# Attention over four images: the search for maxima follows a concave line beside the scores, the next batch's projections are asked for later

## The chip, the cores and the metric

One core of a Trainium2 chip runs the whole program. The metric is the time of the device in microseconds for one execution of the kernel. Five engines work side by side: PE (matrix products), DVE (vector), ACT (scalar functions), POOL and SP, each with its own queue of instructions that it takes in order; semaphores order them among each other.

## What is computed

The program is a network of four layers over four images of 128 channels and 48 x 48 places. The change is in the last attention, which the reference computes so, for B = 4, T = 2304 tokens, 4 heads of 32 channels, all in float32:

```python
qkv = jnp.einsum('btc,oc->bto', x, qkv_w) + qkv_b
q, k, v = jnp.split(qkv, 3, axis=-1)
q, k, v = (heads(q), heads(k), heads(v))
att = jnp.einsum('bhqd,bhkd->bhqk', q, k) * scale
att = jnp.where(causal, att, -jnp.inf)
att = jax.nn.softmax(att, axis=-1)
out = jnp.einsum('bhqk,bhkd->bhqd', att, v)
out = out.transpose(0, 2, 1, 3).reshape(B, T, C)
return jnp.einsum('btc,oc->bto', out, out_w) + out_b
```

x is the layer-normalised stream, and the result is added to it.

## The kernel before, in words

`program` runs six phases one after the other: a selective scan (a), a deformable convolution (b), a linear-attention stack (c), two mixtures of experts (d, f), and between them `attention` (e), which alone is touched. Phases share nothing but X, the stream, which stays on chip.

**Tiling of the attention.** Queries go in blocks n = 0 to 19, five to a batch b (j = 0 to 4, 512 queries wide, the last 256). Keys go in tiles t of 128. A block j has 4(j+1) key tiles (18 for j = 4), of which the last four (two) lie on the diagonal and are narrower. Everything is in the channel layout: a score tile holds 128 keys by up to 512 queries, for four heads in two pairs `hp`, each pair a `slot` of PSUM. There are three slots (two banks each), besides `pO` (outputs) and `pZ` (row sums).

**Kinds of steps.**
- `ln`, `var`, `qk`, `v`: layer norm and projections of group g (512 tokens) of batch b, with `square`, `rstd`, `xn`, `q_out`, `k_out`, `v_out` that take them out of PSUM.
- `most`: the search. For 128 queries i and 512 keys kc, PE forms the scores of two heads the other way round (queries in partitions), and DVE takes their maximum over the keys (`most_out`, L3277; on the diagonal first a mask, L3272). `peak` (L3285) joins the parts, `neg` (L3183) transposes them, and `neg_out` gives minus the maximum of each query, the *level* of block n.
- `score`: four matmuls of K times Q and four that add the level (`e_neg`, `e_ones`); it needs two free slots, and for t = 0 the level of its block (`neg_out`). `masked` on the diagonal (L3291), then `exp` on ACT (L3374) writes P.
- `av` adds into `pO`, `sum` into `pZ`; of four tiles ahead of the diagonal, the first two are added by POOL (`fold`, L3398) so that one `sum` serves both. `rec`, `on`, `proj`, `residual` end the block.

So the level of a block has to be there before its first score tile; the search of a block may run any time after its projections, at most NR = 4 blocks ahead.

**What sets the order.** The order of all steps is worked out when the program is built, by `Line`: jobs (`main` for scores, `outputs`, `others` for projections and search, `projections` for the ends of blocks) are generators on a model clock with a cost for each kind (COST), and each step that a job puts is appended to `ph.order`. Every engine then issues its part of that order, with waits on semaphores. What PE finds first in its queue it must do first.

`others` goes through `plan`: for each block n from 1 the pieces of its search (`max_units`), with projections of the next batch spread among them, and then `neg` n. `done` counts the items gone through. `scores` holds a tile back until `done` has come to `due(n, t)`, which before is the share of the score columns so far, times the weights of the whole plan, less SLACK = 2 items. That binds the scores to the search, but not the search to the scores: `others` runs on as slots permit. Projections of batch b+1 stand in `plan` among the search of blocks j = 1 to 3 (two groups each).

```python
while done[0] < due(n, t) and not stuck[0]:
    yield
```

All matmuls of the phase are issued in the helper `mm`, so that they share line 3129 and are told apart by their tiles: `e_slot<-e_K,e_Q` is the search, `e_slot<-e_Q,e_K` and `e_slot<-e_neg,e_ones` the scores, `e_pO<-e_P,e_V` the outputs, `e_pZ<-e_P,e_ones` the sums, `e_slot<-X,cst` and `e_slot<-e_sqr,cst` the norm, `e_slot<-e_xn,e_w` Q and K, `e_slot<-e_w,e_xn` V, `e_slot<-e_On,e_w` the output projection. Each float32 matmul stands as two instructions in the trace.

Of the kernel before, what the change touches and what calls it, by code (L numbers as in the profile page):

```python
# [14 lines left out]
B, C, HH, WW = 4, 128, 48, 48  # L15
L = HH * WW
# [4 lines left out]
class Phase:  # L21
# [17 lines left out]
    def put(self, kind, *key):  # L39
        self.total[kind] = self.total.get(kind, 0) + 1  # L40
        self.rank[kind, key] = self.total[kind]
        self.order.append((kind, key))
# [11 lines left out]
class Line:  # L54
# [22 lines left out]
    def spawn(self, work):  # L77
        self.jobs.append([self.now[0], work, -1, self.rank[0]])
# [24 lines left out]
    def until(self, kind, *key):  # L103

        while not self.emitted(kind, *key):
            yield
        if self.ready[kind, key] > self.now[0]:
            self.now[0] = self.ready[kind, key]
            yield
# [2717 lines left out]
def attention(nc, A, X, K):  # L2827
    ph = Phase(nc, "e")
    S, upto = ph.sem, ph.upto
    SCALE = float(1.0 / np.sqrt(32))  # L2830
    NT, QB, NP, NR, SLACK = L // 128, 512, 12, 4, 2
    w = ph.sb("w", [128, 384 + 128 + 4])
    cm = ph.sb("cm", [128, 2, 128])
    ones = ph.sb("ones", [128, 128])
# [10 lines left out]
    neg = ph.sb("neg", [128, NR, QB])  # L2845
# [7 lines left out]
    blocks = [(b, j) for b in range(B) for j in range(5)]  # L2853

    def width(j):
        return min(QB, L - j * QB)

    def tiles(j):
        return range(4 * j, 4 * j + width(j) // 128)

    def first(j, t):

        return max(t - 4 * j, 0) * 128

    def key_chunk(i, kc):
        return kc * QB, min((i + 1) * 128, kc * QB + QB)
# [12 lines left out]
    def take(kind, *key, us=None):  # L2879
        while True:  # L2880
            first = min(pairs, default=None, key=lambda x: x[0])
            if len(pairs) <= wanted[0]:
                yield
            elif first[0] > now[0]:
                now[0] = first[0]
                yield
            else:
                break
        pairs.remove(first)
        _, place[kind, key], freed[kind, key] = first  # L2890
        put(kind, *key, us=us)
# [5 lines left out]
    def spread(us, z):  # L2897
        return us * z / QB + .1

    def scores(n, t):  # L2900

        j = blocks[n][1]
        z = width(j) - first(j, t)
        if t == 0:
            yield from until("neg_out", n)
        if tile_no[n, t] >= NP // 2:
            n0, t0 = tile_at[tile_no[n, t] - NP // 2]
            yield from until("av", n0, t0)
            if paired(blocks[n0][1], t0):
                yield from until("fold", n0, t0 // 4 * 4 + 1)  # L2910
            else:
                yield from until("sum", n0, t0)
        while done[0] < due(n, t) and not stuck[0]:
            yield
        wanted[0] = 2
        while len(pairs) < 2 or max(x[0] for x in pairs[:2]) > now[0]:
            if len(pairs) >= 2:
                pairs.sort()
                now[0] = max(now[0], pairs[1][0])
            yield  # L2920
        wanted[0] = 0
        pairs.sort()
        for hp in range(2):
            _, place["score", (n, t, hp)], freed["score", (n, t, hp)] = pairs.pop(0)
        put("score", n, t, us=spread(1.7, z))
        for hp in range(2):
            spawn(weights(n, t, hp, z))
        yield

    def weights(n, t, hp, z):  # L2930
        j = blocks[n][1]
        if t >= 4 * j:
            put("masked", n, t, hp)
            yield
        put("exp", n, t, hp, us=spread(.9, z))
        give(("score", (n, t, hp)), ("exp", (n, t, hp)))
# [44 lines left out]
    def normed(b, g):  # L2981
        put("square", b, g)
        yield
        put("var", b, g)
        yield
        put("rstd", b, g)
        yield
        put("xn", b, g)
        give(("ln", (b, g)), ("xn", (b, g)))

    def query_key(b, g):
        aside("q_out", b, g)
        put("k_out", b, g)
        give(("qk", (b, g)), ("q_out", (b, g)), ("k_out", (b, g)))
        yield

    def out(taker, kind, *key, us=None):
        put(kind, *key, us=us)
        give(taker, (kind, key))
        yield  # L3000

    def extra(kind, *key):
        if kind == "ln":
            b, g = key
            if gno(b, g) >= 2:
                yield from until("v", *divmod(gno(b, g) - 2, 5))
            yield from take("ln", *key)
            spawn(normed(*key))
        elif kind == "qk":
            yield from until("xn", *key)  # L3010
            if key[0] >= 2:
                stuck[0] = True
                yield from until("score", 5 * (key[0] - 1) - 1, NT - 1)
                yield from until("av", 5 * (key[0] - 1) - 1, NT - 1)
                stuck[0] = False
            yield from take("qk", *key)
            spawn(query_key(*key))
        elif kind == "v":
            yield from take("v", *key)
            spawn(out(("v", key), "v_out", *key))  # L3020
        elif kind == "most":
            n, i, kc = key
            b, j = blocks[n]
            a0, a1 = key_chunk(i, kc)
            if kc == 0:
                yield from until("q_out", b, j)
                yield from until("k_out", b, j)
            for hp in range(2):
                yield from take("most", n, i, kc, hp, us=spread(.4, a1 - a0))
                spawn(out(("most", (n, i, kc, hp)), "most_out", n, i, kc, hp,  # L3030
                          us=spread(1.0, a1 - a0) + .43 * (kc == i // 4)))
            if kc == i // 4:
                spawn(top(n, i))
        elif kind == "neg":
            n = key[0]
            j = blocks[n][1]
            for i in tiles(j):
                yield from until("peak", n, i)
            if n >= NR:
                stuck[0] = True  # L3040
                yield from until("score", n - NR, tiles(blocks[n - NR][1])[-1])
                stuck[0] = False
            yield from take("neg", n)
            spawn(out(("neg", key), "neg_out", n))
        yield
# [8 lines left out]
    def top(n, i):  # L3054
        for kc in range(i // 4 + 1):
            for hp in range(2):
                yield from until("most_out", n, i, kc, hp)
        put("peak", n, i)

    def max_units(n):  # L3060
        b, j = blocks[n]
        return [("most", n, i, kc) for i in tiles(j) for kc in range(i // 4 + 1)]

    def others():
        for g in range(5):
            yield from extra("ln", 0, g)
            if g:
                yield from extra("qk", 0, g - 1)
                yield from extra("v", 0, g - 1)
        yield from extra("qk", 0, 4)  # L3070
        yield from extra("v", 0, 4)
        for m in max_units(0):
            yield from extra(*m)
        yield from extra("neg", 0)
        for e in plan:
            yield from extra(*e)
            done[0] += 1

    def gno(b, g):
        return 5 * b + g  # L3080


    plan = []
    for n, (b, j) in enumerate(blocks[1:], 1):
        ahead = []
        if b + 1 < B and 1 <= j < 4:
            ahead += [(kind, b + 1, g) for g in range(2 * j - 2, min(2 * j, 5)) for kind in ("ln", "qk", "v")]
        todo = max_units(n)
        for k, piece in enumerate(ahead):
            todo.insert((k + 1) * (len(todo) + k) // (len(ahead) + 1), piece)  # L3090
        plan += todo + [("neg", n)]
    done, stuck = [0], [False]
    tile_at = [(n, t) for n, (b, j) in enumerate(blocks) for t in range(tiles(j)[-1] + 1)]
    tile_no = {key: k for k, key in enumerate(tile_at)}

    def paired(j, t):
        return t < 4 * j and t % 4 < 2

    WEIGHT = {"ln": 3.0, "qk": 2.0, "v": 1.0, "neg": 1.0}
    work = [sum(width(blocks[m][1]) - first(blocks[m][1], u) for m, u in tile_at[:k]) for k in range(len(tile_at) + 1)]  # L3100
    rest = [sum(WEIGHT.get(e[0], 2.2) for e in plan[:k]) for k in range(len(plan) + 1)]

    def due(n, t):
        share = work[tile_no[n, t]] / work[-1] * rest[-1]
        return max(sum(x <= share for x in rest) - 1 - SLACK, 0)

    line.run((0, main()), (0, outputs()), (0, others()), (0, projections()))

# [293 lines left out]


PHASES = (("a", layer0), ("b", layer1), ("c", layer2a), ("d", experts2), ("e", attention), ("f", experts3))


# [139 lines left out]
```

## Time and profile before

| | |
|---|---|
| time, median of 3 runs | 10961.17 us (10953.19 to 10961.48) |
| the profiled execution | 10953.31 us, its span 10951.5 us |
| instructions | 166018 |
| busy over the span | PE 84%, DVE 70%, ACT 55%, POOL 51% |
| the attention | 9415.3 to 10717.4 us of the span |

The times are those of whole executions. Busy shares are those of the span from the first to the last instruction. The profile also gives the clock that PE was granted, as a share of its full 2.4 GHz; the two levels are 0.5 (1.2 GHz) and 1.

### The profile page before, as it was taken

What the parts mean: (1) busy time and instruction counts of PE and PEld (TensorE: products, weight loads), DVE (VectorE), ACT (ScalarE), POOL (GpSimd) and SP (SyncE); (2) the same over time, 40 slices, a digit from 0 to 9 for tenths busy, and PEclk for the clock granted to TensorE, in tenths of its full rate; (3) what the DMA queues carried; (4) which work ended last, traced back from release to release, by engine and by line L of the source; (5) the groups of instructions that cost most, each with busy time, mean ns of one, the idle gap of its engine ahead of it and who ended that gap; (6) DMA issues with size and microseconds to landing.
All of it is one profiled execution on the core that took longest, in us unless ns stands there. A gap on an engine that the chain in (4) does not pass through costs nothing. (4 is left out here: it accounts for less than half of the span.)

```text
span 10951.5 us, 166018 instructions
## 1 busy us (share of the span) xinstructions
PE 9227.2 (84%) x59866; PEld 4819.9 (44%) x59866; DVE 7622.5 (70%) x8779; ACT 6061.1 (55%) x12476; POOL 5534.4 (51%) x3721
## 2 busy tenths in 40 slices
PE   7888888888888776677798998988989988799897
PEld 3333333333333333566555555555555554333334
DVE  5999999999999996566556665555665653444633
ACT  4666666767666664111356666666666665233233
POOL 5888889889888885666333323222323320011010
PEclk8999999999999998888889999999999999899898
DMA  2222222222222223666300000000000001200003
GB/s 72 76 77 78 80 78 79 79 78 80 78 80 78 79 77 97 193 195 196 102 2 2 4 5 1 4 1 5 4 1 5 1 10 42 94 1 1 1 1 142
DMA packets 259107, 623.72 MB, mean 57 GB/s; under 512 B 26279, under 2 KB 114447, under 8 KB 255992
## 3 DMA queue, kind: packets, MB, share of 16 engines
q1 hardware_dynamic: 203672, 438.27, 12.2%
q0 software_dynamic: 51840, 169.91, 5.2%
q8 instruction: 486, 7.96, 0.3%
q10 hardware_dynamic: 2784, 4.92, 0.1%
q14 instruction: 325, 2.66, 0.1%
HBM read 572.09 MB, written 40.90 MB: 56 GB/s over the span
## 5 line engine op out<-in xcount | busy, mean ns | idle before, releaser
L978 POOL TENSOR_TENSOR a_dBu<-a_du,a_Bs 128x960 f32<-128x960 f32 (+1 forms) x1280 | 2714.5, 2144 | 222.8 <-DVE a_H L750 202.5
L750 DVE TENSOR_TENSOR_SCAN a_H<-a_pA,a_dBu 128x962 f32<-128x962 f32 (+1 forms) x1280 | 2652.6, 2072 | 107.9 <-ACT a_pA L919 54.7
L919 ACT ACTIVATE a_pA<-a_delta,a_al 128x480 f32<-128x480 f32 (+1 forms) x2560 | 1624.8, 639 | 1148.8 <-DVE a_H L750 1143.9
L541 PE MATMUL a_pY<-a_H,cst 128*128 128x480 f32 (+1 forms) x5120 | 2213.5, 554 | 34.4 <-ACT a_Y L936 34.1
L758 DVE TENSOR_TENSOR a_H<-a_H,a_pC 128x960 f32<-128x960 f32 (+1 forms) x1280 | 1393.8, 1089 | 84.3 <-PE a_pC L541 83.0
L541 PEld LDWEIGHTS a_pY<-a_H,cst 128*128 128x128 f32 x5120 | 976.3, 193 | 707.0 <-issue 541.3
L541 PE MATMUL a_pC<-a_stk,a_sel 96*128 96x480 bf16 (+1 forms) x1280 | 471.6, 368 | 512.3 <-DVE a_H L758 504.1
L3398 POOL TENSOR_TENSOR e_P<-e_P 128x1024 f32<-128x1024 f32 (+1 forms) x80 | 151.8, 1918 | 1437.8 <-ACT e_P L3374 1437.8
L1089 POOL DMA_INDIRECT b_gath<-b_tab,b_idx x648 | 613.5, 947 | 392.1 <-issue 176.1
L2459 POOL TENSOR_TENSOR c_KF<-c_KF,c_dg 128x1056 f32<-128x1056 f32 x192 | 386.3, 2013 | 670.7 <-DVE c_MX L2219 670.3
L3374 ACT ACTIVATE e_P<-e_slot 128x1024 f32<-128x1024 f32 (+1 forms) x464 | 347.5, 796 | 657.0 <-PE e_slot L3129 588.5
L541 PEld LDWEIGHTS a_pC<-a_stk,a_sel 96*128 96x128 bf16 x1280 | 124.5, 97 | 1250.5 <-DVE a_H L758 1067.1
L1909 PE MATMUL c_P<-c_U,c_W 128*128 128x384 f32 x1536 | 582.5, 532 | 66.7 <-DVE c_mr L2264 38.5
L1141 PE MATMUL b_pS<-cst,b_gath 128*128 128x128 f32 x2592 | 374.4, 301 | 261.9 <-issue 198.0
L2411 ACT ACTIVATE c_G<-c_P,c_be 128x384 f32<-128x384 f32 x768 | 434.3, 581 | 177.9 <-PE c_P L1909 149.3
L3277 DVE TENSOR_REDUCE e_part<-e_slot 128x2 f32<-128x1024 f32 (+3 forms) x400 | 417.2, 1068 | 165.9 <-PE e_slot L3129 159.7
L1909 PE MATMUL c_P<-c_G,c_W 128*128 128x384 f32 x1536 | 520.9, 493 | 0.1
L2297 DVE SCALAR_TENSOR_TENSOR X<-c_P,c_be,X 128x384 f32<-128x384 f32 x192 | 118.2, 615 | 569.9 <-PE c_P L1909 569.7
L2448 POOL TENSOR_TENSOR c_t<-c_t 128x384 f32<-128x384 f32 x192 | 194.5, 1013 | 620.1 <-DVE c_t L2215 619.5
L2206 DVE SCALAR_TENSOR_TENSOR c_t<-c_P,c_be,c_sincos 128x384 f32<-128x384 f32 x576 | 335.5, 610 | 228.5 <-PE c_P L1909 226.3
L1141 PEld LDWEIGHTS b_pS<-cst,b_gath 128*128 128x128 f32 x2592 | 341.6, 211 | 296.6 <-issue 265.1
L2244 DVE TENSOR_REDUCE c_KS<-c_KF 128x264 f32<-128x1584 f32 x128 | 375.5, 2949 | 109.3 <-ACT c_KF L2370 109.2
(468 smaller groups left out, 18043.8 us busy)
## 6 DMA issues: line engine op xcount, KB each, us to landing
a_Bs<-a_brows SPq DMA_DIRECT2D x512, 480.0 KB
a_Bs<-a_brows SPq DMA_DIRECT2D x128, 384.0 KB
d_W<-in_d_w SPq DMA_DIRECT2D x32, 1024.0 KB, 7.5
f_W<-in_f_w SPq DMA_DIRECT2D x32, 1024.0 KB, 7.8
b_tab<-b_TT SPq DMA_DIRECT2D x32, 576.0 KB
b_gath<-b_tab,b_idx POOLq DMA_INDIRECT x648
a_zt<-a_sz SPq DMA_DIRECT2D x36, 256.0 KB
a_sz<-a_zt SPq DMA_DIRECT2D x16, 480.0 KB
```

The source lines that it names most:

```text
L541: return pe.matmul(out, lhsT, rhs, start=start, stop=stop, skip_group_check=True)
L750: v.tensor_tensor_scan(span(H[:, g % NH, :], g), factors(g), span(dBu[:, g % ND, :], g), 0.0, ALU.mult, ALU.add).then_inc(S(kind), 1)
L758: v.tensor_tensor(inner(H[:, g % NH, :], g), inner(H[:, g % NH, :], g), pC[:, 0:z].unsqueeze(1).broadcast_to([128, 2, z]), ALU.mult).then_ ...
L919: s.activation(pA[:, k, at:at + z], delta[:, u % 2, h, 0:z], ACT.Exp, scale=al[:, o + 2 * d, h, n:n + 1]).then_inc(S(kind), 1)
L978: g.tensor_tensor(inner(dBu[:, i % ND, :], i), du[:, u % 2, :, 0:z], Bs[:, p % NB, i % 2, 0:z].unsqueeze(1).broadcast_to([128, 2, z]), ALU ...
L1089: g.indirect_dma_start(out=gath[:, n % NG, t, :], out_offset=None, in_=tab[b], in_offset=bass.IndirectOffsetOnAxis(ap=idx[:, b % 2, j * 9 ...
L1141: m = pe.matmul(pS[:, place[kind, key], (t % 4) * 128:(t % 4 + 1) * 128], gath[:, n % NG, t, q * 128:(q + 1) * 128], ident, start=q == 0, ...
L1909: return pe.matmul(out, lhsT, rhs, start=start, stop=stop, skip_group_check=True)
L2244: v.tensor_reduce(KS[:, i, :], KF[:, :, i, :, :].rearrange("p c g m -> p (g m) c"), AX.X, ALU.add).then_inc(S(kind), 1)
L2411: s.activation(G[:, c % 2, j, :], half("up", n, c // 2 * 2, 0)[:, j, 0:CH], ACT.Gelu, bias=bias(n, 3 + j)).then_inc(S(kind), 1)
L2459: g.tensor_tensor(KF[:, c, :, :, :], KF[:, c, :, :, :], dg[:, c % 2, :].rearrange("p (i g) -> p i g", i=4).unsqueeze(3).broadcast_to([128, ...
L3277: v.tensor_reduce(part[:, n % NR, i - 4 * j, 2 * hp:2 * hp + 2, kc], sl[:, :, 0:z], AX.X, ALU.max).then_inc(S(kind), 1)
```

## The change

It is in the planner alone; what the steps do and the buffers are as before.

- Each level n has a latest point: EARLY = 1024 score columns before its block begins, by which the plan up to `neg` n has to be done (`corners`). `path` is the concave line from the origin over these points (from each point on to the next with the steepest rise). `due` reads it in place of the straight share.
- Scores wait until `done` is at least `due` less SLACK, as before, and now `others` waits while `done` is more than `due` plus SLACK (`reached` holds the `due` of the tile in hand).
- Projections of batch b+1 stand in the plan among the search of blocks j = 3 (groups 0 to 2) and j = 4 (groups 3 and 4).

```diff
-    NT, QB, NP, NR, SLACK = L // 128, 512, 12, 4, 2
+    NT, QB, NP, NR, SLACK, EARLY = L // 128, 512, 12, 4, 2, 1024
...
         z = width(j) - first(j, t)
+        reached[0] = due(n, t)
         if t == 0:
...
-        while done[0] < due(n, t) and not stuck[0]:
+        while done[0] < reached[0] - SLACK and not stuck[0]:
             yield
...
         for e in plan:
+            while done[0] > reached[0] + SLACK:
+                yield
             yield from extra(*e)
             done[0] += 1
...
-        if b + 1 < B and 1 <= j < 4:
-            ahead += [(kind, b + 1, g) for g in range(2 * j - 2, min(2 * j, 5)) for kind in ("ln", "qk", "v")]
+        if b + 1 < B and j >= 3:
+            ahead += [(kind, b + 1, g) for g in ((0, 1, 2), (3, 4))[j - 3] for kind in ("ln", "qk", "v")]
...
-    done, stuck = [0], [False]
+    done, reached, stuck = [0], [0], [False]
...
+    opened = [plan.index(("neg", n)) + 1 for n in range(1, len(blocks))]
+    corners = [(max(work[tile_no[n, 0]] - EARLY, 0), rest[k]) for n, k in enumerate(opened, 1)]
+    path, at = [(0, 0)], (0, 0)
+    while at[1] < rest[-1]:
+        at = max((p for p in corners if p[1] > at[1]), key=lambda p: ((p[1] - at[1]) / max(p[0] - at[0], 1), p[1]))
+        path.append(at)
+
     def due(n, t):
-        share = work[tile_no[n, t]] / work[-1] * rest[-1]
-        return max(sum(x <= share for x in rest) - 1 - SLACK, 0)
+        share = np.interp(work[tile_no[n, t]], [x for x, _ in path], [y for _, y in path])
+        return max(sum(x <= share for x in rest) - 1, 0)
```

How it moves the work on PE is seen in two places. A row is a run of equal matmuls; x2 of `e_slot<-e_K,e_Q` is one piece of search (two heads), x4 two pieces.

The first is block 14 (batch 2, j = 4), from its first score tile. Before:

```order
8292 L3129 MATMUL e_slot<-e_Q,e_K 128x256 x4
8293 L3129 MATMUL e_slot<-e_neg,e_ones 128x256 x4
8294 L3129 MATMUL e_pO<-e_P,e_V 32x128 x4
8295 L3129 MATMUL e_slot<-e_K,e_Q 128x512 x2
8296 L3129 MATMUL e_pZ<-e_P,e_ones 32x128 x4
8297 L3129 MATMUL e_slot<-e_K,e_Q 128x512 x10
8298 L3129 MATMUL e_pO<-e_P,e_V 32x256 x4
8299 L3129 MATMUL e_slot<-e_K,e_Q 128x128 x4
8300 L3129 MATMUL e_slot<-e_K,e_Q 128x512 x12
8301 L3129 MATMUL e_slot<-e_K,e_Q 128x256 x4
8302 L3129 MATMUL e_slot<-e_K,e_Q 128x512 x12
8303 L3129 MATMUL e_slot<-e_K,e_Q 128x384 x4
```

The same place after the change:

```order
8305 L3139 MATMUL e_slot<-e_Q,e_K 128x256 x4
8306 L3139 MATMUL e_slot<-e_neg,e_ones 128x256 x4
8307 L3139 MATMUL e_pO<-e_P,e_V 32x128 x4
8308 L3139 MATMUL e_slot<-e_K,e_Q 128x512 x2
8309 L3139 MATMUL e_pZ<-e_P,e_ones 32x128 x4
8310 L3139 MATMUL e_slot<-e_K,e_Q 128x512 x2
8311 L3139 MATMUL e_slot<-e_Q,e_K 128x256 x4
8312 L3139 MATMUL e_slot<-e_neg,e_ones 128x256 x4
8313 L3139 MATMUL e_slot<-e_K,e_Q 128x384 x2
8314 L3139 MATMUL e_pO<-e_P,e_V 32x256 x4
8315 L3139 MATMUL e_slot<-e_K,e_Q 128x384 x2
8316 L3139 MATMUL e_pO<-e_P,e_V 32x256 x4
```

The run of 32 pieces behind the first score tile is gone; two pieces stand there, and two behind the next.

The second is block 8 (batch 1, j = 3), which before holds no search at all:

```order
7902 L3129 MATMUL e_slot<-e_Q,e_K 128x512 x4
7903 L3129 MATMUL e_slot<-e_neg,e_ones 128x512 x4
7904 L3129 MATMUL e_pO<-e_P,e_V 32x128 x4
7905 L3129 MATMUL e_pZ<-e_P,e_ones 32x128 x4
7906 L3129 MATMUL e_slot<-e_Q,e_K 128x512 x4
7907 L3129 MATMUL e_slot<-e_neg,e_ones 128x512 x4
7908 L3129 MATMUL e_pO<-e_P,e_V 32x512 x4
7909 L3129 MATMUL e_slot<-e_On,e_w 128x512
7910 L3129 MATMUL e_slot<-e_Q,e_K 128x512 x4
```

After:

```order
7891 L3139 MATMUL e_slot<-e_Q,e_K 128x512 x4
7892 L3139 MATMUL e_slot<-e_neg,e_ones 128x512 x4
7893 L3139 MATMUL e_pZ<-e_P,e_ones 32x128 x4
7894 L3139 MATMUL e_slot<-e_K,e_Q 128x512 x2
7895 L3139 MATMUL e_slot<-e_xn,e_w 128x512 x2
7896 L3139 MATMUL e_slot<-e_Q,e_K 128x512 x4
7897 L3139 MATMUL e_slot<-e_neg,e_ones 128x512 x4
7898 L3139 MATMUL e_slot<-e_K,e_Q 128x512 x2
7899 L3139 MATMUL e_pO<-e_P,e_V 32x512 x4
7900 L3139 MATMUL e_slot<-e_K,e_Q 128x512 x2
7901 L3139 MATMUL e_slot<-e_On,e_w 128x512
7902 L3139 MATMUL e_pO<-e_P,e_V 32x512 x4
```

Search and the projections of batch 2 now stand between its score tiles. The search there is that of blocks 9 to 11.

## Rows read from the trace of the kernel before

**Rows 1.** The page: span, and busy time by engine.
```profile
span 10951.5 us, 166018 instructions
PE 9227.2 (84%) x59866; PEld 4819.9 (44%) x59866; DVE 7622.5 (70%) x8779; ACT 6061.1 (55%) x12476; POOL 5534.4 (51%) x3721
```

**Rows 2.** Windows (stretch, length, busy: PE, PEld, DVE, ACT, POOL; PEclk, DMA): attention.
```profile
9415.30:10717.40 1302.10, 1182.99 (x9122) 455.60 (x9122) 583.09 (x843) 436.74 (x625) 151.75 (x80) 0.92 0.01 1
```

**Rows 3.** Windows: blocks 0-3, 4, 5-7, 10-15, cut at first exponentials.
```profile
9464.10:9749.30 285.20, 256.60 (x1722) 91.67 (x1724) 142.57 (x202) 89.09 (x118) 27.96 (x12) 0.92 0.00 1
9749.30:9788.80 39.50, 37.68 (x563) 20.24 (x563) 3.51 (x8) 20.20 (x39) 9.96 (x8) 1.00 0.01 2
9788.80:10015.10 226.30, 201.45 (x1234) 74.23 (x1236) 137.46 (x193) 59.03 (x84) 13.95 (x6) 0.90 0.00 1
...
10110.70:10551.40 440.70, 402.10 (x2768) 152.19 (x2772) 252.82 (x350) 115.10 (x168) 37.92 (x20) 0.88 0.00 1
```

**Rows 4.** Windows: blocks 16 (j=1), 17 (j=2), 18 (j=3), without search.
```profile
10551.40:10578.70 27.30, 25.65 (x254) 9.24 (x257) 4.50 (x10) 14.19 (x19) 4.67 (x2) 1.00 0.01 2
10578.70:10620.80 42.10, 40.05 (x374) 13.70 (x374) 4.50 (x10) 21.88 (x27) 9.34 (x4) 1.00 0.00 1
10620.80:10676.80 56.00, 53.55 (x494) 18.07 (x494) 4.50 (x10) 29.59 (x34) 14.00 (x6) 1.00 0.01 1
```

**Rows 5.** Timeline of PE (start, length); and the tile e_slot: transposes.
```profile
9703.19 1.07 PE L3129 MATMUL e_pO<-e_P,e_V 128*32 128x512 f32 x8
9704.07 1.04 PE L3129 MATMUL e_pZ<-e_P,e_ones 128*32 128x512 f32 x8
9705.05 1.13 PE L3129 MATMUL e_slot<-e_sqr,cst 128*128 128x512 f32 x2
9706.10 1.07 PE L3129 MATMUL e_pZ<-e_P,e_ones 128*32 128x512 f32 x8
...
L3183 PE MATMUL e_slot<-cst,e_peak x72: 272/273/475, 9456.0 to 10549.1; 128*128 128x128 f32 x72
```

**Rows 6.** Groups of DVE in the attention (busy us, mean ns | idle before).
```profile
L3277 DVE TENSOR_REDUCE e_part<-e_slot 128x2 f32<-128x1024 f32 (+3 forms) x400 | 417.2, 1068 | 165.9 <-PE e_slot L3129 159.7
L3272 DVE TENSOR_TENSOR e_slot<-e_slot,e_cm 128x256 f32<-128x256 f32 x144 | 61.2, 425 | 44.9 <-PE e_slot L3129 44.3
```

**Rows 7.** Windows: the run of 17 in block 6, that of 32 in block 14.
```profile
9870.90:9899.00 28.10, 24.28 (x121) 9.62 (x118) 22.38 (x30) 4.20 (x8) 0.00 (x0) 0.88 0.00 1
10436.00:10478.50 42.50, 40.80 (x171) 16.66 (x170) 38.43 (x46) 2.31 (x4) 0.00 (x0) 0.60 0.00 1
```

**Rows 8.** Waits in 9418 to 10725 (us in total, times, longest).
```profile
PEld e_slot L3129 <- DVE e_part L3277: 206.0, 241, 2.5
PE e_slot L3129 <- DVE e_part L3277: 41.3, 83, 1.6
```

**Rows 9.** Windows: block 6 tiles 0-6, its twin; block 12 tiles 0-4, its twin.
```profile
9830.10:9870.90 40.80, 38.33 (x288) 14.70 (x290) 19.48 (x30) 16.68 (x21) 4.66 (x2) 1.00 0.01 1
10551.40:10576.20 24.80, 23.18 (x230) 8.30 (x233) 4.29 (x10) 13.43 (x17) 4.67 (x2) 1.00 0.01 1
10219.90:10250.50 30.60, 27.87 (x192) 9.41 (x194) 12.85 (x15) 10.81 (x13) 4.65 (x2) 1.00 0.00 1
10578.70:10598.30 19.60, 17.99 (x158) 5.84 (x158) 1.44 (x2) 10.78 (x12) 4.67 (x2) 1.00 0.00 1
```

**Rows 10.** Timeline of PE: one search piece between output and row sum.
```profile
9602.69 1.07 PE L3129 MATMUL e_pO<-e_P,e_V 128*32 128x512 f32 x8
9603.69 1.13 PE L3129 MATMUL e_slot<-e_K,e_Q 32*128 32x512 f32 x4
9604.75 1.06 PE L3129 MATMUL e_pZ<-e_P,e_ones 128*32 128x512 f32 x8
```

**Rows 11.** Windows: tile 3 of block 6 and of block 16.
```profile
9846.80:9853.70 6.90, 6.90 (x56) 2.65 (x52) 1.78 (x3) 2.58 (x4) 0.00 (x0) 1.00 0.01 2
10562.60:10566.90 4.30, 4.30 (x40) 1.35 (x44) 0.48 (x2) 1.94 (x2) 0.00 (x0) 1.00 0.00 0
```

## Prediction

> **What bounds the kernel now.** I read the page first: span and busy shares [rows 1]. The time of the profiled execution is 10953.3 us, its span 10951.5. The change touches only the attention, whose instructions run from 9415.3 to 10717.4, 1302.1 us, 12% of the span [rows 2]. There PE is busy 1183.0 us, DVE 583.1, ACT 436.7, POOL 151.8, and PE's granted clock is 0.92 on average. So PE sets the pace, but not at its full clock. Between the two levels of 1.2 and 2.4 GHz, a mean of 0.92 is 16% of the phase at 1.2 GHz, about 210 us.
>
> Then I cut the phase at the start of the first exponential of each query block [rows 3]. Three stretches hold all search for maxima after the lead-in; between and behind them stand blocks of scores alone. Without search PE has clock 1.00 and DVE nearly nothing to do. With search DVE works for half the time or more and the clock is 0.92, 0.90 and 0.88. The work is bunched: the search runs far ahead, then stops.
>
> **Price of the search now.** My unit is one search piece of 512 keys for two heads. The 400 reductions of the phase are 342 units (175104 columns over 512, counted over the PE's order), 3584 of those columns in the lead-in, so 335 units behind it. The three stretches last 285.2 + 226.3 + 440.7 = 952.2 us. The same blocks without search take 27.3 us (j=1), 42.1 (j=2), 56.0 (j=3) [rows 4], 39.5 (j=4) [rows 3]. A block j=0 nowhere stands alone; going by columns at the price of j=1, which is 8.2 ns, its 1280 would take 10.5 us, and smaller blocks pay more per column, so I take 12. Blocks 0 to 3: 137.4; 5 to 7: 81.4; 10 to 15: 188.9; sum 407.7. That leaves 544.5 us. In them lie the projections of batches 1 to 3. A group's matmul of 512 columns holds PE some 1.0 us (9705.05 to 9706.10; I take V's four small ones as one) [rows 5], five of them to a group, 4.5 groups to a batch: 13.5 x 5.0 = 68 us. The 19 groups of transposes of the levels (up to four of 0.27 us that overlap, [rows 5]) I put at 0.6 each, 11 us. The search then costs 544.5 - 68 - 11 = **466 us, 1.39 us a unit**.
>
> **Where that price comes from.** In a long run of search DVE is the pace: 417.2 us of reductions and 61.2 of masks [rows 6] over 342 units are 1.40 us a unit. Measured: the run of 17 pieces that ends block 6 takes 28.1 us [rows 7] against 2.5 in block 16 (27.3 of [rows 4] less 24.8 of [rows 9]); less 5.1 for the projections, transposes and output that lie in it, 20.5 us for 15 units, 1.37. That of 32 in block 14 takes 42.5; less 2.2 for its score tile (39.5 us for 18) and 1.0 for the output projection, 39.3 for 29 units, 1.36 [rows 7]. DVE is busy 22.4 and 38.4 us in them, and the clock is 0.88 and 0.60. PE waits for DVE's reductions 206.0 us before weight loads and 41.3 before matmuls [rows 8]. What stands behind a run pays too, since its score matmuls still run at the low clock.
>
> **Price of a spread piece.** Now stretches in which at most five pieces stand between two score tiles, against the same tiles of batch 3 [rows 9]. Block 6, tiles 0 to 6: 40.8 against 24.8, 16.0 more. In it are the matmuls of ln, of var twice, Q, K and V (6.0), and the output projection has moved out of it (1.0): 11.0 us for 10.5 units, 1.05. Block 12, tiles 0 to 4: 30.6 against 19.6, 11.0 more, with half-width var, Q and K for 1.5 and again 1.0 moved out: 10.5 for 9 units, 1.17. Together 21.5 / 19.5 = **1.10**. The clock is 1.00 in both although they hold 0.26 and 0.29 units per us. The single piece shows why: from 9603.69 to 9604.75 it holds PE 1.06 us between an output matmul and a row sum [rows 10], and its reduction on DVE (1.07 us on average, [rows 6]) lies beside other work.
>
> **The change, part by part.** No engine gets an instruction more or less. (1) `due` follows the concave line through the latest points at which each level must be ready, and `others` holds back beyond SLACK. By the PE's order, 41 of 68 gaps of the old program that hold search have at most four pieces, but runs of eight or more take 218.5 units. The new one has 151 gaps with search, none of seven to nine pieces, three of ten with 26.5 units, and 306 units in gaps of one to six. 81 score tiles have none, where 164 had. The lead-in takes 9.5 units instead of 7. (2) The projections of the next batch are asked for with the search of blocks j=3 and j=4, which comes well ahead of their scores. They keep their matmuls. I cost them at nothing more: by the order, the last V of a batch stands some 27 score tiles ahead of its first use, and ACT has room (busy 29.6 of 56.0 us in a pure block, [rows 4]). If that cover went, each group would hold the search for its chain of ln, square, var, rstd, xn, some 5 us, four times at worst. (3) The new wait of `others` is one of the planner, not of the chip; what stands behind it is the search of later blocks. Its risk is a level that is ready too late: the new order puts the transposes at least 1280 columns before their block (384 for block 1), over two tiles and 6 us, against a chain reduction - peak - transposes - copy of about 3 us. Before, six blocks had them directly ahead of their first scores. I take 0 for this, -10 to +10 as bounds.
>
> Sum after: 306 x 1.10 = 337, 26.5 x 1.40 = 37, together 374, against 466: -92. The lead-in, where nothing hides it, +3. **-89 us**, so 10864 for the profiled execution. The median of the runs shown is 10961.2, 8 above it: **10872**. Bounds of the price: 1.18, about that of the second stretch, gives -65; 0.95 gives -135: two pieces of different heads that run side by side would hold PE as long as one, 0.53 each, and 0.95 is what comes out if a fifth of them do.
>
> The order also costs something. PE changes between 32-row and 32-column tiles of the array more often: 806 changes of shape instead of 708. From an output matmul to a row sum of the same shape it is 0.88 us (9703.19 to 9704.07, [rows 5]), from an output matmul to a search piece 1.00 (9602.69 to 9603.69, [rows 10]). The Trainium skill, TensorEngine Tiling (Array Packing), Tiling Modes, says that changing the tiling mode drains the engine. The trace agrees with some 0.1 us; by that rule 98 more changes would be about 10 us, and the sum -79. I leave it out, since the stretches that give 1.10 have such changes themselves.
>
> **The clock.** From 10436.0 to 10478.5 PE is busy 40.8 of 42.5 us and has 0.60 [rows 7]; in 10551.4 to 10578.7 it is busy 25.7 of 27.3 and has 1.00 [rows 4]. So busy time alone does not keep the clock. The pure stretches of [rows 3] have 1.00 throughout, the falls lie where search is, and the runs have them most. I expect the 210 us at 1.2 GHz to shrink to about 70. The Trainium skill, TensorE: Matmul & The Clock Gate, Part 1, tells of a clock that is held down by default and that activity releases; taken as busy time, it would deny that this change helps the clock, which is the first rival.
>
> **Rivals.** (a) The clock stays low as long as now. What speaks for it: spread or bunched, a search piece fills half of the array. Against it: both stretches of [rows 9]. The 140 us that I let go would stay at half clock, and work bound by PE gives half of it back: -89 + 70 = -19, 10942, no change. Chance 0.07. (b) Slower: slots. A score tile needs two of three slots at once, and each piece put before it holds one until DVE has reduced it. A single piece can so cost more than one in a run: from 9846.8 to 9853.7 one piece and V take 6.9 us against 4.3 in block 16 [rows 11], less 1.0 for V, 1.6 us for the unit. If all 306 cost that the sum is 490 + 37 + 3 = 530, +64: 11025. The change stops paying at 1.39 and is slower by over 0.2% from 1.46. Against it: the stretches of [rows 9] have such pieces in them. Chance 0.05. (c) More gain: pieces side by side and the clock at 1.00 throughout, 0.95 a unit, -135: 10826. Chance 0.10. (d) That the planner's order hardly changes is excluded by the two orders.
>
> **How the numbers follow.** My forecast has 0.78, at 10872 with 10835 to 10925 as its own bounds. A measurement of this kernel tells about 0.2%, 22 us, from no change. Faster by more: 0.78 + 0.10 = 0.88; within 0.2%: 0.07; slower: 0.05. For 8 in 10 the range takes in half of (c) and ends below (a): 10828 to 10935.
>
> **What would show it.** The attention lasts 1195 to 1235 us; its clock is 0.96 or more; DVE is busy 583 us again; the last stretches without search, of batch 3, become longer (they get search), while blocks 14 and 15 shrink from 79.0 and 36.4 us; PE's waits for reductions fall from 247.3 us (206.0 and 41.3) to under 120. Wrong would be a mean clock of 0.92 again (rival a), or PE's waits for DVE as long as now at clock 1.00 (rival b).

## The result, and the profile after

Five runs each, on one chip: before 10961.48 us (10953.19 to 10972.68), after 10896.53 us (10882.21 to 10912.05). The ratio is 0.9941, with a 95% interval of 0.9930 to 0.9952: 65 us or 0.6% faster. 10872 was forecast, with 10828 to 10935 as range: the direction, the range and its inner bounds held; the gain was a quarter smaller than the 89 us forecast. Of all runs below, two executions stand apart at a lower clock, one of av_sum (11414.73 us, clock 0.819) and one of before on the third chip (18927.01 us, clock 0.5), and the ratios, and av_sum's median, are without them.

The profiled execution has a span of 10894.7 us. The windows of its attention, as whole and by pieces (stretch, length, busy us of PE, PEld, DVE, ACT and POOL, clock, DMA), answer to [rows 2], [rows 3] and [rows 4]: the phase, the lead-in, block 4, block 8, and blocks 13 to 19:

```profile
9416.80:10658.30 1241.50, 1137.52 (x9122) 432.57 (x9122) 592.23 (x843) 436.04 (x625) 151.78 (x80) 0.97 0.01 1
9416.80:9470.20 53.40, 41.36 (x158) 20.52 (x158) 25.35 (x44) 16.28 (x28) 0.00 (x0) 0.77 0.03 8
9755.00:9817.50 62.50, 58.20 (x640) 27.13 (x641) 33.06 (x46) 19.75 (x37) 9.97 (x8) 1.00 0.01 2
9953.00:10056.80 103.80, 92.80 (x692) 33.95 (x692) 54.79 (x83) 34.91 (x45) 14.00 (x6) 0.98 0.00 1
10259.10:10349.70 90.60, 82.07 (x632) 30.08 (x630) 40.30 (x66) 32.79 (x43) 13.98 (x6) 0.98 0.00 1
10349.70:10418.30 68.60, 61.55 (x652) 28.18 (x652) 31.98 (x44) 20.98 (x40) 9.99 (x8) 0.95 0.01 1
10418.30:10437.50 19.20, 17.30 (x154) 6.17 (x155) 11.92 (x19) 5.93 (x10) 0.00 (x0) 1.00 0.00 1
10437.50:10480.90 43.40, 40.84 (x338) 15.18 (x338) 24.52 (x33) 15.86 (x22) 4.67 (x2) 1.00 0.01 2
10480.90:10550.60 69.70, 65.21 (x466) 21.13 (x466) 36.52 (x44) 21.23 (x25) 9.32 (x4) 1.00 0.00 1
10550.60:10617.30 66.70, 63.02 (x547) 21.09 (x544) 18.26 (x28) 29.91 (x35) 14.00 (x6) 1.00 0.00 1
10617.30:10658.30 41.00, 36.86 (x551) 19.77 (x548) 3.88 (x8) 20.97 (x40) 9.96 (x8) 0.98 0.01 2
```

The attention lasts 1241.5 us, 60.6 less than before, where 89 less was forecast; that is also above the 1195 to 1235 us that the prediction gave as a sign of being right. DVE's work is the same but for 9 us (592.2 for 583.1). The clock is 0.97 for 0.92: the time at 1.2 GHz, summed from the clock's records, fell from 210 us to 74. Blocks 14 and 15 shrank from 79.0 and 36.4 us to 68.6 and 19.2, and blocks 16 to 18 grew from 27.3, 42.1 and 56.0 to 43.4, 69.7 and 66.7, since they now hold search.

The waits in the attention (us in total, times, longest), against [rows 8]:

```profile
PEld e_slot L3139 <- DVE e_part L3287: 125.7, 150, 2.9
PE e_slot L3139 <- DVE e_part L3287: 44.5, 67, 2.1
```

Together 170 us, where 247 stood before and under 120 was forecast. That is where the missing part of the gain has to be looked for. The gain itself has two sides that no run here takes apart: PE waits 77 us less, and it is 136 us less at 1.2 GHz, which is worth up to 68 us where its matmuls set the pace. Together that is more than the 60.6 us gained, so the two overlap.

### The profile page after: what moved, and what is told of

Same layout as the page of the kernel before. It is cut to its first block and busy times, and to the rows that moved or that the text cites. A ratio compares the mean times of both kernels' runs of the same rounds, so it can differ in the third digit from the quotient of the medians.

```text
span 10894.7 us, 166020 instructions
## 1 busy us (share of the span) xinstructions
PE 9174.6 (84%) x59866; PEld 4794.5 (44%) x59866; DVE 7631.1 (70%) x8779; ACT 6057.8 (56%) x12476; POOL 5534.8 (51%) x3721
```

## The experiments

The kernels ran on three chips (proj_only, pace_only and the two light ones on the first; av_sum, early_256, slack_1 and cost_real on the second; the last four on the third), so each is set against the runs of before on its own chip. The attention is compared by its own length in the profiled execution, across chips too, since the kernel before was profiled once. That length is a better yardstick than the whole, since the other phases vary: on the chip of the last four kernels the deformable convolution (phase b, with its gathers) takes 871 us, in the other traces 1034 to 1051, and on one chip the phases ahead of the attention end up to 23 us apart. The same order twice (on two chips) gave 1241.5 and 1238.4 us, another order 1213.0 and 1219.1; so a difference of 6 us or less tells nothing.

### Which part of the change does it

**proj_only**: the old kernel with the new places of the projections.

```diff
-        if b + 1 < B and 1 <= j < 4:
-            ahead += [(kind, b + 1, g) for g in range(2 * j - 2, min(2 * j, 5)) for kind in ("ln", "qk", "v")]
+        if b + 1 < B and j >= 3:
+            ahead += [(kind, b + 1, g) for g in ((0, 1, 2), (3, 4))[j - 3] for kind in ("ln", "qk", "v")]
```

> The old kernel with the projections of the next batch asked for later, and the old straight share without the hold back. By the order, 202 of the 342 units still stand in gaps of seven pieces or more. Theory A (runs of search are what costs, through DVE's pace and the low clock): within 0.1% of before, 10961 +-12. Rival B (the projections in the old places stole the room of the search): a third or more of the 65 us is here, 10940 or less.

Measured: 10943.88 us against 10945.67 for before, ratio 0.9999 (0.9989 to 1.0009); the attention 1298.4 us for 1302.1, clock 0.91. Nothing moved: rival B falls. (The 10961 and 10940 expected stand on before's time on the other chip; against 10945.67 they would be some 16 us lower.)

**pace_only**: the changed kernel with those two lines put back.

```diff
-        if b + 1 < B and j >= 3:
-            ahead += [(kind, b + 1, g) for g in ((0, 1, 2), (3, 4))[j - 3] for kind in ("ln", "qk", "v")]
+        if b + 1 < B and 1 <= j < 4:
+            ahead += [(kind, b + 1, g) for g in range(2 * j - 2, min(2 * j, 5)) for kind in ("ln", "qk", "v")]
```

> The changed kernel with the projections where they stood before, so the concave line and the hold back alone. By the order, 262 units stand in gaps of one to six pieces and 72.5 in longer ones (changed kernel: 306 and 26.5). Theory A: the gain goes by the units moved out of long runs, (218.5 - 72.5) / (218.5 - 26.5) = 76% of it, about 10912. Rival B: a third or less is here, 10940 or more.

Measured: 10885.8 us, ratio 0.9946 (0.9929 to 0.9962); the attention 1263.5 us, 38.6 less than before. Here are the windows of its attention and, second, of proj_only's:

```profile
9408.10:10671.60 1263.50, 1152.94 (x9122) 437.86 (x9122) 592.23 (x843) 435.83 (x625) 151.80 (x80) 0.96 0.01 1
```

```profile
9389.80:10688.20 1298.40, 1194.48 (x9122) 460.10 (x9122) 582.93 (x843) 436.65 (x625) 151.78 (x80) 0.91 0.01 1
```

By the attention, the pacing alone gives 64% of the gain (76% was expected), the projections alone next to nothing, and both together 22 us more than the pacing. The orders differ as one would expect for that: 72.5 units in gaps of seven pieces and more, against 26.5 with both and 218.5 before. A likely reason is that, with the projections in their old places, the search cannot be held back as far, since it stands behind them in the plan; no run tests it. By the whole this split isn't seen: the medians give the pacing alone 60 us on its chip, where 49 were expected, and its interval overlaps with that of both together. Its profiled execution, at 10908.18 us, was the slowest of its four.

### What a run of search costs, and what a spread piece costs

**before_light** and **after_light**: the old and the changed kernel, in which a reduction reads the first quarter of the keys of its piece. The levels are then maxima over a part of the keys. PE has the same matmuls in the same order. DVE keeps the masks, and the reduction of a whole piece takes 0.42 us instead of 1.22, so this shortens DVE's part and does not take it away.

```diff
-                    v.tensor_reduce(part[:, n % NR, i - 4 * j, 2 * hp:2 * hp + 2, kc], sl[:, :, 0:z], AX.X,
+                    v.tensor_reduce(part[:, n % NR, i - 4 * j, 2 * hp:2 * hp + 2, kc], sl[:, :, 0:z // 4], AX.X,
```

> The old kernel in which each reduction of the search reads only the first quarter of its keys, so the levels are maxima over a part of the keys; PE's work and the order are the same. It takes DVE's pace out of the runs. Theory A: the runs of 17 and of 32 fall from 28.1 and 42.5 us to what PE needs for its pieces, 1.06 us or less each, some 23 and 33 us. Of the clock: if PE's waits for DVE pull it down, the attention's mean rises from 0.92 to 0.97 or more; if half-filled array does, it stays at 0.92 or below. The attention takes 1302 us before: with the clock up about 1190, with the clock as now about 1240.

> The changed kernel with the same quarter reductions (levels over a part of the keys). Its attention takes 1241.5 us, 27 us more than the 1213 that I forecast, since a unit costs 1.21 instead of 1.10 us. Theory C (the rest is PE's own: a piece alone holds PE 1.06 us, and the array changes its shape more often): the attention stays within 10 us, 1232 to 1242. Theory D (the rest is slots that wait for DVE): it falls by 25 us or more, to 1216 or less.

Measured: 10775.64 and 10790.55 us, one run each. First the windows of before_light: the attention, the run of 17, the run of 32, tiles 0 to 6 of block 6 and tiles 0 to 4 of block 12, in the places of [rows 2], [rows 7] and [rows 9], and the lead-in:

```profile
9400.20:10537.90 1137.70, 1051.36 (x9122) 424.04 (x9122) 319.39 (x843) 436.83 (x625) 151.76 (x80) 0.98 0.01 2
9808.20:9828.80 20.60, 19.01 (x132) 8.32 (x122) 11.23 (x30) 4.25 (x9) 0.00 (x0) 1.00 0.00 1
10287.50:10310.30 22.80, 22.49 (x170) 10.43 (x169) 16.35 (x46) 2.36 (x5) 0.00 (x0) 1.00 0.00 1
9769.50:9808.20 38.70, 36.90 (x282) 14.17 (x286) 11.48 (x30) 16.69 (x21) 4.66 (x2) 1.00 0.01 1
10110.40:10139.40 29.00, 25.84 (x192) 9.15 (x194) 5.75 (x15) 10.84 (x14) 4.65 (x2) 1.00 0.00 1
9400.20:9445.10 44.90, 37.01 (x142) 18.16 (x142) 15.81 (x37) 16.89 (x29) 0.00 (x0) 0.83 0.03 9
```

The attention of after_light and its lead-in:

```profile
9398.90:10552.30 1153.40, 1080.18 (x9122) 421.44 (x9122) 327.12 (x843) 435.70 (x625) 151.79 (x80) 1.00 0.01 2
9398.90:9442.40 43.50, 35.01 (x158) 18.40 (x158) 17.88 (x44) 16.30 (x28) 0.00 (x0) 0.90 0.04 10
```

The waits for reductions that are left, in before_light and then in after_light, and four pieces of the run of 32 in before_light:

```profile
PEld e_slot L3129 <- DVE e_part L3277: 89.3, 146, 1.7
PE e_slot L3129 <- DVE e_part L3277: 9.1, 18, 0.9
PEld e_slot L3139 <- DVE e_part L3287: 47.8, 68, 1.8
PE e_slot L3139 <- DVE e_part L3287: 8.8, 15, 1.0
10289.70 2.58 PE L3129 MATMUL e_slot<-e_K,e_Q 32*128 32x512 f32 x16
```

Four things follow.

1. **The gain was DVE's pace in the runs, with the low clock that came along.** With short reductions the old order needs 1137.7 us instead of 1302.1, and the run of 32 falls from 42.5 to 22.8 us. All that the change gains, and more, is in DVE's hold on PE. It fell further than the 1190 us expected with the clock up, and the runs further than 23 and 33 us; the second point says why.
2. **Take that away and the change loses.** With short reductions the new order is 15.7 us longer than the old one (1153.4 to 1137.7). Its spread pieces cost PE more. By the sum of the prediction, the new order then pays 1153.4 - 43.5 (lead-in) - 4 x 176.9 (scores of a batch, 12 + 27.3 + 42.1 + 56.0 + 39.5) - 68 - 11 (projections, transposes) = 323 us for 332.5 units, 0.97. The old order pays 1137.7 - 44.9 - 4 x 176.9 - 68 - 11 = 306 us for 335 units, 0.91. The difference comes from its runs. Of that of 32, 22.8 less 2.2 and 1.0 leaves 19.6 us for 29 units, 0.68 a unit, and four whole pieces in it take 2.58 us, 0.65 each, where one alone holds PE 1.06 us [rows 10]. The matmuls of two pieces, heads 0, 1 and heads 2, 3, overlap there: four of them start within 0.02 us at 10289.70.
3. **By the bounds set beforehand theory C falls and D holds, but this run alone does not explain the 27 us.** The changed kernel loses 88 us of its 1241.5 when the reductions are short, where C allowed 10. Of its 1.21 us a unit, 0.24 go with the length of the reductions. But the 1.10 held such a part too: in before_light the two stretches behind it take 38.7 and 29.0 us, which leaves 8.9 + 8.9 us for 19.5 units, 0.91. So 0.19 of the 1.10 went with the length, and of the 0.11 that the price was short, 0.05 does and 0.06 (0.97 less 0.91) does not. What is in the 0.06, the masks and slots that still make PE wait (56.6 us in after_light, 0.17 a unit, for 0.12 in the two stretches of before_light) or PE's own work, these two kernels cannot tell; cost_real below narrows it.
4. **The clock fell with PE's waiting; a half-filled array alone does not bring it down.** In before_light the same matmuls in the same runs have the clock at 1.00, where the run of 32 had 0.60; the time at 1.2 GHz is 36 us, and 8 in after_light. DVE's reductions are the only thing that was made faster.

Where DVE holds PE in the changed kernel is seen behind tile 9 of block 13. The timeline of PE (start, length, in brackets the idle time before and what ended it), then that of DVE:

```profile
10311.85 1.06 PE L3139 MATMUL e_pO<-e_P,e_V 128*32 128x512 f32 x8
10312.84 0.68 PE L3139 MATMUL e_slot<-e_K,e_Q 32*128 32x128 f32 x8
10314.33 0.70 PE L3139 MATMUL e_slot<-e_K,e_Q 32*128 32x256 f32 x4 [0.81 <-DVE e_part L3287]
10314.96 1.07 PE L3139 MATMUL e_pO<-e_P,e_V 128*32 128x512 f32 x8
10315.95 1.35 PE L3139 MATMUL e_slot<-e_K,e_Q 32*128 32x256 f32 x12
10319.34 2.09 PE L3139 MATMUL e_slot<-e_Q,e_K 32*128 32x512 f32 x8 [2.04 <-DVE e_part L3287]
```

```profile
10313.38 0.43 DVE L3282 TENSOR_TENSOR e_slot<-e_slot,e_cm 128x256 f32<-128x256 f32 x1 [12.23 <-PE e_slot L3139]
10313.85 0.42 DVE L3287 TENSOR_REDUCE e_part<-e_slot 128x2 f32<-128x256 f32 x1
10314.19 0.42 DVE L3282 TENSOR_TENSOR e_slot<-e_slot,e_cm 128x256 f32<-128x256 f32 x1
10314.65 0.43 DVE L3287 TENSOR_REDUCE e_part<-e_slot 128x2 f32<-128x256 f32 x1
10315.08 0.43 DVE L3282 TENSOR_TENSOR e_slot<-e_slot,e_cm 128x256 f32<-128x256 f32 x1
10315.54 0.69 DVE L3287 TENSOR_REDUCE e_part<-e_slot 128x2 f32<-128x512 f32 x1
10316.15 0.15 DVE L3295 TENSOR_REDUCE e_peak<-e_part 128x4 f32<-128x4 f32 x1
10316.70 0.43 DVE L3282 TENSOR_TENSOR e_slot<-e_slot,e_cm 128x256 f32<-128x256 f32 x1 [0.40 <-PE e_slot L3139]
10317.17 0.69 DVE L3287 TENSOR_REDUCE e_part<-e_slot 128x2 f32<-128x512 f32 x1
10317.78 0.42 DVE L3282 TENSOR_TENSOR e_slot<-e_slot,e_cm 128x256 f32<-128x256 f32 x1
10318.24 0.96 DVE L3287 TENSOR_REDUCE e_part<-e_slot 128x2 f32<-128x768 f32 x1
10319.11 0.42 DVE L3282 TENSOR_TENSOR e_slot<-e_slot,e_cm 128x256 f32<-128x256 f32 x1
10319.57 0.96 DVE L3287 TENSOR_REDUCE e_part<-e_slot 128x2 f32<-128x768 f32 x1
```

Six pieces stand here in one gap. They are 3 units by their columns, but all lie on the diagonal, so that each has a mask of 0.43 us and its semaphore in front of the reduction. DVE needs some 7 us for them, from 10313.38 to 10320.53, PE stands still for 2.04 us before the next score tile, and the clock falls: the tile's matmuls take 2.09 us where 1.14 is usual. From the first exponential of tile 9 to that of tile 10 it is 10.9 us, and 8.2 in after_light.

### What is left: shape changes, places, prices

**av_sum**: the changed kernel, row sum straight behind the output matmuls.

```diff
                 put("av", n, t, us=spread(.85, z))
-                yield
                 if not paired(j, t):
```

> The changed kernel in which the planner puts the row sum straight behind the output matmuls of a tile, so that no search piece stands between them. The array changes shape 633 times instead of 806, below even the 708 of the old kernel. If a change of shape costs what the rule gives, 0.1 us each, the attention gains 17 us against 1241.5. Theory D (what is left above 1.10 us a unit is PE waiting for DVE's reductions in three slots): pieces now stand closer together, and the attention gets slower, 1245 or more.

Measured: 10897.27 us, ratio 0.9939 (0.9918 to 0.9959); the attention 1246.9 us at clock 0.95. Its waits for reductions:

```profile
PEld e_slot L3138 <- DVE e_part L3286: 147.8, 181, 2.9
PE e_slot L3138 <- DVE e_part L3286: 52.5, 77, 2.1
```

The waits rose by 30 us, and the time at 1.2 GHz from 74 to 121 us, as D says, but the phase grew by 5 us only. Something gave back about as much. 173 fewer changes of shape at 0.1 us, an estimate from two starts in the trace, would be 17 us and might fit, but this kernel moves two things at once, and it does not show it. The 17 us less that shape changes alone would have given did not come.

**early_256**: `EARLY` 256 instead of 1024.

```diff
-    NT, QB, NP, NR, SLACK, EARLY = L // 128, 512, 12, 4, 2, 1024
+    NT, QB, NP, NR, SLACK, EARLY = L // 128, 512, 12, 4, 2, 256
```

> The changed kernel with EARLY 256 instead of 1024: levels may be done half a tile ahead of their block. By the order 15.5 units are left in gaps of seven and more (26.5). Theory D: some 3 to 5 us less than 1241.5 by the shorter runs, unless the levels come late; a level that is late shows as PE waiting for the copy of the level, and 10 us or more on top.

Measured: 10879.51 us, ratio 0.9923 (0.9907 to 0.9940); the attention 1241.2 us. No gain in the phase itself, where D expected 3 to 5 us, so the lower ratio is not the attention's. PE's score matmuls wait four times for the copy of a level, 2.3 us in all (0.9 in the changed kernel, 3.7 before): that part of the prediction's risk, priced at nothing, stays small even with a quarter of the lead.

**slack_1**: `SLACK` 1 instead of 2.

```diff
-    NT, QB, NP, NR, SLACK, EARLY = L // 128, 512, 12, 4, 2, 1024
+    NT, QB, NP, NR, SLACK, EARLY = L // 128, 512, 12, 4, 1, 1024
```

> The changed kernel with SLACK 1: the search is held within one item of the line instead of two. By the order 138.8 units stand in gaps of four to six (81.8) and 180.8 in gaps of one to three (224.2). Theory D: more pieces close together, so 5 to 15 us above 1241.5; if only runs of seven and more count (15.0 units instead of 26.5), some 4 us below.

Measured: 10907.98 us, ratio 0.9956 (0.9941 to 0.9971); the attention 1252.6 us, 11 more. This agrees with D: gaps of four to six pieces cost, not only those of seven and more. The intervals of the whole overlap; the 11 us rest on the attention. PE's waits for reductions are 205 us (148.0 and 57.1).

**cost_real**: the planner's prices of a piece as the trace has them.

```diff
-            "most": ("PE", .5), "most_out": ("DVE", 1.07), "peak": ("DVE", .2), "neg": ("PE", .6), "neg_out": ("ACT", .6),
+            "most": ("PE", 1.0), "most_out": ("DVE", 1.25), "peak": ("DVE", .2), "neg": ("PE", .6), "neg_out": ("ACT", .6),
...
-                yield from take("most", n, i, kc, hp, us=spread(.4, a1 - a0))
+                yield from take("most", n, i, kc, hp, us=spread(.9, a1 - a0))
                 spawn(out(("most", (n, i, kc, hp)), "most_out", n, i, kc, hp,
-                          us=spread(1.0, a1 - a0) + .43 * (kc == i // 4)))
+                          us=spread(1.15, a1 - a0) + .43 * (kc == i // 4)))
```

> The changed kernel with the search priced in the planner as the trace has it: 1.0 us on PE and 1.25 on DVE for a piece instead of 0.5 and 1.07. By the order 236 units stand in gaps of one to three (224), 14.5 in gaps of seven and more (26.5), 58 tiles have none (81). Theory D: PE waits for DVE shrink, the attention is 10 to 20 us below 1241.5. Theory that the planner's prices do not matter: within 5 us.

Measured: 10875.58 us, ratio 0.9923 (0.9906 to 0.9941); the attention 1213.0 us, 28.5 less than the changed kernel's, just what the prediction had for that one:

```profile
9426.30:10639.30 1213.00, 1124.58 (x9122) 431.27 (x9122) 594.64 (x843) 435.50 (x625) 151.75 (x80) 0.98 0.01 1
```

Its waits, against 125.7 and 44.5:

```profile
PEld e_slot L3139 <- DVE e_part L3287: 99.6, 141, 2.6
PE e_slot L3139 <- DVE e_part L3287: 24.3, 38, 1.9
```

The waits for reductions fell by 46 us and the time at 1.2 GHz from 74 to 43. D holds, and the planner's prices matter. This is also the run that bears most on the 27 us: it has the same pieces and the same masks as the changed kernel, and by PE's order 805 changes of shape for its 806. Yet by the prediction's sum its search costs 1213.0 - 54.1 (lead-in) - 4 x 176.9 - 68 - 11 = 372 us, 1.12 a unit for 1.21 (1.14 by the second trace of this kernel, below). So neither the number of shape changes nor the diagonal pieces as such made the price of the changed kernel; how closely its pieces stand did.

The last four kernels set the best against the changed one on one chip, five executions each. **cost_pe** has of cost_real's edits only the `us=spread(.9, a1 - a0)` of `most`; **cost_e256** has cost_real's and `EARLY` 256.

```diff
-                yield from take("most", n, i, kc, hp, us=spread(.4, a1 - a0))
+                yield from take("most", n, i, kc, hp, us=spread(.9, a1 - a0))
```

> The changed kernel again, on the same chip as the three that follow: 0.994 of before.

> The planner with the search at the trace's prices again. Its attention took 1213.0 us against 1241.5: on one chip the whole should stand some 28 us below the changed kernel, 0.9915 of before.

> The same prices with EARLY 256. By the order 20.0 units in gaps of seven and more (14.5), 56 tiles without search (58). Alone EARLY 256 left the attention where it was (1241.3). I expect it within 5 us of the kernel with the prices alone.

> Of the prices only the one on PE is put right (1.0 us for a piece), DVE's stays at 1.07. If the planner put pieces too close because it believed that PE is held 0.5 us by each, this alone gives most of the 28 us: attention 1220 or less. If it is DVE's price, it stays at 1235 or more.

| kernel | median us | ratio to before (95%) | attention us | at 1.2 GHz, us |
|---|---|---|---|---|
| before | 10778.9 | 1 | | |
| after_again | 10711.62 | 0.9938 (0.9924 to 0.9952) | 1238.4 | 68 |
| cost_real_again | 10699.07 | 0.9924 (0.9910 to 0.9938) | 1219.1 | 53 |
| cost_e256 | 10692.29 | 0.9919 (0.9905 to 0.9933) | 1217.9 | 64 |
| cost_pe | 10700.01 | 0.9934 (0.9920 to 0.9948) | 1224.6 | 66 |

The changed kernel repeats its ratio. The three with truer prices have attentions 14 to 21 us shorter, less than the 28 above, and medians 12 to 19 us lower; their intervals still overlap with the changed kernel's. The price on PE alone gives 14 of the 19 us of both. That points at the planner's belief that a piece holds PE for half a microsecond as what set pieces too close; but between 1220 and 1235, the result fits neither of the two bounds set beforehand, so it is not settled. cost_e256 stays within 5 us of the prices alone, as expected. It has the lowest median, but its interval overlaps with that of the changed kernel too.

## Why the prediction was right, and where its size was off

- **What bounds the kernel.** Right. PE sets the pace, DVE bounds the runs of search and the clock falls in them: before_light shows it, and pace_only that moving pieces out of runs gains.
- **Price before, 1.39 us a unit, DVE's 1.40 in a run.** Right as a sum. The runs collapse from 28.1 and 42.5 us to 20.6 and 22.8 with short reductions.
- **Price after: the term that failed.** 1.10 a unit was forecast. Measured, by the same sum: 1241.5 - 53.4 - 4 x 176.9 - 68 - 11 = 401 us for 332.5 units, **1.21**. That is 27 us more than the 374 of the prediction. The step was to take 1.10 from two stretches of the old kernel. Two things were wrong with it. The stretches were as friendly as the old kernel had them: PE waits for reductions 5.6 us in them, 0.29 a unit, and 170 us in the changed kernel, 0.50 a unit. In the new order two of three tiles have search. cost_real, which sets the same pieces further apart with as many changes of shape, comes down to 1.12 (1.14 in its second trace), which is 23 to 29 us less; so the closeness of the pieces is shown as the larger part. And the unit went by columns, while DVE's hold of a slot goes by pieces too: over the changed kernel's attention, masks and their semaphores included, a whole piece costs DVE 1.22 us a unit (256 units) and the 144 diagonal ones 2.11 (86 units). Of all pieces 36% are diagonal, in the two stretches 6 of 23, so those were the cheaper kind; how many of the 27 us this is, no run shows.
- **Lead-in.** +3 was forecast, 4.6 came (53.4 for 48.8).
- **The shape changes of the array.** Left out of the sum, as worth 10 us at most. That term would have brought the forecast nearer, but by luck if at all: cost_real has the 1213 us of the forecast with 805 such changes for 806, and av_sum is unclear. What a change costs stays open.
- **The clock.** 70 us at 1.2 GHz was forecast, 74 came. No sum stood behind the 70, so the close agreement is luck; that it would fall by far was right. Rival (a) falls. Its ground, that a search piece fills half of the array wherever it stands, is answered by before_light: the same half-filled runs keep 2.4 GHz once PE does not wait. The busy share misleads here, since at 1.2 GHz a matmul takes nearly twice as long (2.09 us for 1.14 above) and so looks busy: the run of 32 is busy to 96% at a clock of 0.60. The Trainium skill, TensorE: Matmul & The Clock Gate, Part 1, says that activity releases the clock; before_light agrees with that in so far as a PE that waits less keeps 2.4 GHz.
- **Projections at nothing.** Right: 0.9999 for them alone. Together with the pacing they are worth some 22 us by the attention, which was not foreseen.
- **Levels that come late, -10 to +10.** Right at nothing: PE's score matmuls wait 0.9 us for levels, 2.3 with EARLY 256.
- **Rival (b), slots.** It did not decide, but its mechanism, PE held by slots that wait for DVE, is the one that cost_real points to for the 27 us: PE's waits for DVE fell to 170 us, not below 120. A price of 1.39 would have been needed for no gain.
- **Rival (c), 0.95 a unit.** It did not come; even with short reductions the new order pays 0.97. Two pieces side by side cost 0.65 to 0.68 us each in before_light, not the 0.53 that the prediction took for them.

## What to carry to other kernels

Spreading work over a long phase pays if it takes a second engine's pace out of runs, and it has a price of its own on the first engine: take the second engine's part away (here by shorter reductions in both orders) to see both, as the order that is better now was 16 us worse then. A price has to be read from a stretch that is as dense as the new program will be, and per instruction as well as per column. A planner's prices are worth checking against the trace: putting those of one piece right shortened the attention by another 19 to 28 us, where the change gave 61.

## What was not expected of the hardware

- The same matmuls in the same order run at 0.60 or at 1.00 of the full clock (the run of 32: 42.5 and 22.8 us), by whether the reductions that free their PSUM slots take 1.22 us or 0.42 for a whole piece.
- Search pieces of different heads, back to back, hold PE 0.68 us a unit in a run of before_light, against 1.06 us for one alone between other work.
- The phase of the deformable convolution, which no kernel here changes, took 871 us in the four traces of one chip and 1034 to 1051 on the others; before itself had a median of 10778.9 us there and 10961.5 here. What in the phase differs was not looked into.
